# The last token tile of a Mamba block with a mixture of experts: expert picks, gate logits, ranks and GpSimd products stand elsewhere

## The reference, cut to what matters

```python
xz = einsum('bld,ed->ble', x, W_in); xs, z = split(xz)
xc = silu(causal_conv4(xs) + conv_b)
a = softplus((xc @ W_x.T)[..., :32] @ W_dt.T + b_dt)
out = (xc * a * silu(z)) @ W_out.T + x
x1 = layernorm(x + out)
scores = sigmoid(x1 @ gate_w.T); sfc = scores + gate_bias
# 4 groups of 4 experts: the 2 groups with the largest sum of their top 2 stay,
# of those the 4 best experts; their weights are scores, normalized, times 2.5
y = sum over the token's experts e of cw[e] * (silu(x1 @ Wg[e].T) * (x1 @ Wu[e].T)) @ Wd[e].T
y += (silu(x1 @ Ws_g.T) * (x1 @ Ws_u.T)) @ Ws_d.T
x2 = layernorm(x1 + x1 + y)
```

## Time and profile before

| | us |
|---|---|
| median of 3 runs | 582.47 (579.99 to 583.5) |
| the profiled execution | 584.27 |
| its span on the core | 582.5 |
| TensorE busy | 527.9 (91%) |
| VectorE busy | 434.3 (75%) |
| ScalarE busy | 373.3 (64%) |
| GpSimd busy | 332.1 (57%) |

### The profile page before, as it was taken

One profiled execution on the slowest core, in us unless ns is written; L12 is line 12 of the kernel. 1 busy time (PEld: TensorE's weight loads), 2 busy tenths in 40 slices (PEclk: granted clock), 3 DMA queues, 4 the chain that ended last, 5 costly groups with the idle time before them and its releaser, 6 DMA issues.

```text
span 582.5 us, 11734 instructions
## 1 busy us (share of the span) xinstructions
PE 527.9 (91%) x3112; PEld 442.9 (76%) x3112; DVE 434.3 (75%) x1103; ACT 373.3 (64%) x960; POOL 332.1 (57%) x368
## 2 busy tenths in 40 slices
PE   6878899899999999999859898999999998899782
PEld 5667486686867778676648798899999998889661
DVE  4886599998999999999895577434353558887666
ACT  4693858858486683855622576677777776676561
POOL 2412113277575766856576667777777766666720
PEclk9988999999999999999988999999999999999997
DMA  7992403234142422313695647977676688883986
GB/s 163 309 292 81 153 36 110 73 120 152 62 148 83 154 98 94 132 52 108 214 384 189 225 155 245 329 243 220 195 212 196 196 302 289 294 299 128 360 316 228
DMA packets 70182, 111.21 MB, mean 191 GB/s; under 512 B 12676, under 2 KB 52997, under 8 KB 69608
## 3 DMA queue, kind: packets, MB, share of 16 engines
q1 hardware_dynamic: 53624, 71.38, 38.7%
q0 software_dynamic: 13056, 35.68, 16.7%
q10 hardware_dynamic: 3440, 3.41, 1.7%
HBM read 61.77 MB, written 50.74 MB: 193 GB/s over the span
## 4 chain that ended last, share of the span: by engine, by line
PE 46%; DVE 31%; issue 10%; ACT 5%; DMA 4%; POOL 3%; POOLq 0%; SPq 0%; ACTq 0%; DVEq 0%
PE psum L928 6%; DVE xc L1366 6%; PE psum L929 5%; PE psum L930 5%; PE psum L910 5%; PE psum L731 4%; DVE sp L1388 3%; PE psum L952 3%; PE psum L954 3%; PE psum L953 3%; PE psum L938 2%; POOL x_buf L620 2%; DVE m L1392 2%; PE psum L706 2%; PE psum L670 1%
## 5 line engine op out<-in xcount | busy, mean ns | idle before, releaser
L620 POOL DMA_INDIRECT x_buf<-row,row_id x128 | 131.4, 1026 | 64.6 <-issue 36.2
L662 POOL DMA_INDIRECT y_buf<-y_out,y_ids x96 | 95.8, 998 | 47.1 <-issue 26.9
L612 POOL TENSOR_TENSOR m<-xc,zs 128x512 f32<-128x512 f32 x32 | 41.5, 1317 | 90.1 <-DVE shift L1428 44.5
L1736 DVE TENSOR_TENSOR t_lo<-psum,t_hi 128x512 fp32r<-128x512 f32 x72 | 48.8, 685 | 55.6 <-ACT t_hi L1215 55.6
L928 PE MATMUL psum<-ew_gu_hi,t_hi 128*128 x288 | 84.8, 295 | 2.6 <-issue 0.8
L929 PE MATMUL psum<-ew_gu_lo,t_hi 128*128 x288 | 81.7, 284 | 0.0
L930 PE MATMUL psum<-ew_gu_hi,t_lo 128*128 x288 | 81.4, 283 | 0.0
L1366 DVE SCALAR_TENSOR_TENSOR xc<-psum,cw_taps,xc 128x511 f32<-128x511 f32 (+2 forms) x96 | 71.5, 747 | 7.2 <-ACT halo_x L1055 4.9
L928 PEld LDWEIGHTS psum<-ew_gu_hi,t_hi 128*128 128x128 f32 x288 | 54.8, 190 | 6.8 <-issue 5.8
L731 PE MATMUL psum<-wout,m 128*128 128x256 f32 x224 | 53.2, 398 | 3.7 <-DVE m L1392 3.1
L929 PEld LDWEIGHTS psum<-ew_gu_lo,t_hi 128*128 128x128 f32 x288 | 55.0, 191 | 0.2
(11 more groups left out here) (241 smaller groups left out, 1347.6 us busy)
## 6 DMA issues: line engine op xcount, KB each, us to landing
tiles_in<-x_buf SPq DMA_DIRECT2D x144, 144.0 KB
y_in<-y_buf SPq DMA_DIRECT2D x32, 512.0 KB, 6.2
xT<-in_x_T SPq DMA_DIRECT2D x8, 512.0 KB, 3.7
xtok<-in_x_tok SPq DMA_DIRECT2D x8, 512.0 KB, 3.6
gu_hi_buf<-w_hi_now SPq DMA_DIRECT2D x8, 512.0 KB, 3.7
out_dram<-res ACTq DMA_DIRECT2D x6, 512.0 KB, 5.6
x_buf<-pad_row SPq DMA_DIRECT2D x17, 144.0 KB
raw_gu<-in_wg_T SPq DMA_DIRECT2D x16, 128.0 KB, 3.6
```

Source lines behind the costliest of these rows:

```text
L620: nc.gpsimd.indirect_dma_start(out=x_buf, out_offset=bass.IndirectOffsetOnAxis(ap=row_id[t % ROWS][:, b, k:k + 1], axis=0), in_=row[t % RO ...
L662: nc.gpsimd.indirect_dma_start(out=y_buf, out_offset=bass.IndirectOffsetOnAxis(ap=y_ids[:, q % IDS, i:i + 1], axis=0), in_=y_sent[:, i, :] ...
```

## The change

Five edits, all on the last tile:

1. GpSimd: ahead of chunks 2 and 3 of tile 7's product the wait for `y_done` is gone. The waits for `wout_mm`, `xc_done` and `z_evac` stay.
2. `gate(7)` writes its logits to PSUM bank 4, which held the turned rows of tile 7 and is free once the gate's inputs are read; `gate_out(7)` reads them there. `gate_turn` still writes to bank 3.
3. So `gate(7)` no longer waits for `routed` = 7. That wait now stands ahead of `gate_turn(7)`.
4. TensorE: `ranks(6)` stands behind `gate_up(0, 0)`, `gate(7)` and `turn_x(0, 1)`, directly ahead of `shared_up(7, 0)`.
5. VectorE: `pick(6)` stands behind the layer norm, `shared_act(6, 1)` and the low parts of the first quad; `x1T_low(7)` stands ahead of `choose(6)`.

```diff
--- before.py
+++ after.py
@@ -381,6 +381,10 @@
             if c < 2:
                 return 4 + c
             return c - 2 if t == NT - 1 else 4 + c if t == 0 else 2 + c
+
+        def gate_bank(t):
+
+            return 4 if t == NT - 1 else 3
 
         def z_bank(c):
 
@@ -632,7 +636,8 @@
 
             def tile(t, sends=True, first=False, halos=True, last=False):
                 if not first:
-                    at_least(pool, "y_done", PAIRS * t + 1)
+                    if not last:
+                        at_least(pool, "y_done", PAIRS * t + 1)
                     gate_product(t, range(2, KI))
                 if sends:
                     send(t - 2, range(0, 2))
@@ -758,9 +763,7 @@
                 at_least(pe, "x1T_h", KD * (t + 1))
                 at_least(pe, "x1T_l", KD * (t + 1))
                 at_least(pe, "z_evac", KI * min(t + 2, NT))
-                if t == NT - 1:
-                    at_least(pe, "routed", t)
-                o = psum[0:2 * E, 3, :]
+                o = psum[0:2 * E, gate_bank(t), :]
                 for k in range(KD):
                     pe.matmul(o, gw_split[:, k, :], x1T_hi[:, k, :], start=k == 0, stop=False)
                     mm = pe.matmul(o, gw_split[:, k, :], x1T_lo[:, k, :], start=False, stop=k == KD - 1)
@@ -1006,11 +1009,12 @@
             shared_up(t - 1, 1)
             transposes(t)
             shared_down(t - 1)
-            ranks(t - 1, t)
             gate_up(0, 0, tile_experts(0))
             gate(t)
             turn_x(0, 1)
+            ranks(t - 1, t)
             shared_up(t, 0)
+            at_least(pe, "routed", t)
             gate_turn(t)
             each_quad(iteration)
             down(0, NQ - 1, tile_experts(NQ - 1))
@@ -1102,7 +1106,7 @@
 
             def gate_out(t):
                 at_least(act, "logit_mm", t + 1)
-                A(logits[:, :], psum[0:2 * E, 3, :], ACT.Copy).then_inc(s["logit_out"], 1)
+                A(logits[:, :], psum[0:2 * E, gate_bank(t), :], ACT.Copy).then_inc(s["logit_out"], 1)
 
             def gate_exp(t):
                 at_least(act, "gate_sum", t + 1)
@@ -1842,15 +1846,15 @@
                 weights_low(i)
             route(t - 1)
             shared_act(t - 1, 0)
-            pick(t - 1)
             norm_in(t, range(0, 2))
             layer_norm(t)
             shared_act(t - 1, 1)
             at_least(dve, "w_stored", 16 * PIECES)
             for k in range(KD):
                 turned_low(0, 0, k)
+            pick(t - 1)
+            x1T_low(t)
             choose(t - 1)
-            x1T_low(t)
             place(t - 1)
             residual(t - 1)
             each_quad(iteration)
```

## The result

The changed kernel takes **586.84 us** (median of 5 runs, 585.65 to 586.88) against 582.47 us (5 runs, 579.99 to 583.5): a ratio of 1.0077, 95% interval 1.0053 to 1.0102. It is slower by 4.4 us, and it lies outside the range that ended at 585.4. The profiled execution took 586.84 us, its span 585.1 us against 582.5. The lines of code have moved: L1534 was L1530, L1451 was L1447, L675 was L670, L1546 was L1542.

A forecast was written before the change was run, and what follows sets the result against it. VectorE was taken to bound the stage before tile 7's transposes, TensorE what follows. 2.6 us gained ahead of the turn and 2.6 given back behind the ranks, plus 0.4 for the clock: 582.9 us, range 579.3 to 585.4.

The forecast's parts named there:

- The picks behind the norm: VectorE, tile 6's pick: 2.13 us come out from ahead of tile 7's layer norm.
- The product without its wait: GpSimd, tile 7: second m gains 1.35 us, less 0.85 from contention with VectorE, so 0.5 us.
- one whole half: Upper bound on VectorE's delay at posn: waiting for one whole half of GpSimd's product, 1.27 us.
- The clock: TensorE's idle gaps ahead of tile 7's transposes and behind the ranks: cases -2.3, 0, +2.3 us; 0.4 added.
- As today: Likeliest of three clock cases on TensorE: slow matmuls cost the same as before, 0 us.
- The ranks behind the turn: TensorE ahead of shared_up(7, 0): the round trip to the residual, covered before, becomes bare, costing 2.6 us.
- "slower" rival: The gap ahead of shared_up(7, 0) also drops TensorE's clock, 2.3 us more: 585.2 us, chance 0.2.
- The other bank, the sends, the weights: gate(7) in bank 4, GpSimd's sends, expert weight loads: each 0 us, the weights with 3 us of cover.
- L1546 stretched to about 1 us: Sign of being right: VectorE's posn step of tile 5, held by the product; 0.22 us would mean wrong.

The follow-up runs named there:

- h2: Kernel before with only tile 6's pick moved behind the layer norm (x1T_low ahead of choose): 579.78 us, ratio 0.9934.
- f2: Kernel before with only chunk 2 of tile 7's product freed of its wait, chunk 3 keeping it: ratio 1.0004 on a 673 us chip.
- e1: Kernel before with only the wait ahead of tile 7's product (chunks 2 and 3) removed: ratio 0.998 on a 673 us chip.
- f1: Kernel before with only the wait ahead of tile 7's product removed, measured again: ratio 1.0004 on a 673 us chip.
- f3: Changed kernel plus 22 calls of unread identity products on TensorE behind the ranks: ratio 1.0073 on a 673 us chip.
- g1: The changed kernel again, unaltered, against the kernel before on another chip: 587.03 us, ratio 1.0117.
- h1: Kernel before with only the wait ahead of tile 7's product removed: 585.03 us, ratio 1.0038.
- g3: Changed kernel with tile 7's product waiting for the last step of choose(5) instead of not waiting: 583.05 us, ratio 1.0027.
- g4: Kernel before with the picks moved and tile 7's product waiting for the last step of choose(5): 578.06 us, ratio 0.9947.
- g2: Changed kernel with the product's y_done wait put back: 583.15 us, ratio 1.0017.
- i2: Kernel before with only the picks moved behind the norm: ratio 1.0068 on a 673 us chip.

## Why the prediction was wrong

- **The picks behind the norm: right, but the number it was to be seen by came out by luck.** The picks alone took the idleness ahead of the transposes from 6.29 to 3.73 us. For the whole change the forecast was 3.3 us and the measurement 3.19, though the norm was not ready 2.6 us earlier: its last step started 0.57 us later than before (302.10 against 301.53). The idle stretch shrank all the same because TensorE reached it later still. Behind `gate_turn(6)` VectorE gained the picks' 2.13 us and the whole 1.35 us at the second `m`, not 0.5, since `posn` was not held; and TensorE gained 0.43 us, since the output projection ran through, where the forecast had taken 0.4 us off the idle time for its later end. So 6.29 - 2.13 - 1.35 + 0.43 = 3.24 us, near the 3.19 measured: the two errors, each of about 0.85 us, cancel.

```profile
302.10 0.16 DVE L1432 SCALAR_TENSOR_TENSOR shift<-mv,rstd 128x4 f32<-128x4 f32 x1
```

  What the picks alone give, -0.66%, is more than the 2.1 us: the slow clock behind a shorter idle stretch costs less too (6.07 us for transposes and `shared_down(6)` in h2 against 7.10).
- **The product without its wait: this step failed.** The forecast took 0.85 us of contention at `posn` (bounds 0 to 1.27) and let nothing ahead of it suffer. It was 2.95 us, at L1534, for two reasons. It looked for the victim only among the steps that start behind the product's shown start (281.4): L1530 at 280.82 [0.22 us] was through by then. In fact the step that started 0.57 us ahead of the product's shown start was held. And the bound of "one whole half" was wrong, since the halves stand back to back and the step waited for both (3.17 us, against 1.95 with one half in f2). Behind it came what the forecast never priced: the residual of tile 5, the first thing that TensorE waits for in this stretch, with TensorE already idle for 0.90 us ahead of it. So 2.95 us went straight into TensorE's time.
- **The clock: the right mechanism at one place too few.** Two places were weighed (transposes, ranks' gap), and both showed a lower clock. The third, ahead of `shared_up(6, 0)`, cost +2.42 us, because the stall made it. "As today" held roughly for the sum of the other two: -1.38 and +1.49.
- **The ranks behind the turn: gap right, weight too small.** 2.69 us against 2.6. But the forecast booked the clock there as a rival of 0.2, at 2.3 us; it cost 1.49. Alone, this move costs 0.71%, 4.1 us. Its "slower" rival (585.2 us, to which the range adds 0.2 us without a source) was the right mechanism, and came on top of the stall that the sum did not hold.
- **The other bank, the sends, the weights: right.** No wait on weights in the changed kernel, and the sends moved without being waited for. The wait for `ew_d_hi` stays at its size:

```profile
336.28 0.38 PE L955 MATMUL psum<-ew_d_hi,a_hi 128*128 x1 [1.17 <-DMA ew_d_hi<-d_hi_buf]
```

- **What should have been asked.** The forecast's own test, "L1546 stretched to about 1 us", was refuted: 0.22 us. The product's start was given as 281.4, behind a send on GpSimd, and that was right (280.12 in an execution 1.28 us ahead). The last step of `choose(5)`, L1530 with two inputs in SBUF, lies 0.58 to 0.36 us ahead of it. No row that the forecast had said that a step so far ahead can be held, so this is hindsight; but a margin of half a microsecond around a start that is itself an estimate would have put L1530 on the list of victims. The bound would then have been 2.5 + 0.6 = 3.1 us in place of the 0.85 taken, and the range would have reached 585.4 + 2.25 = 587.6 us.

The Trainium skill, "SBUF — State Buffer", "Who interferes with whom", says that a VectorE instruction with two SBUF inputs contends with a GpSimd instruction that reads SBUF, that the shared ports are an exclusive lock, and that issue order decides who is blocked. The trace agrees (3.17 us for a step of 0.22, no delay at all for the residual with one input in PSUM). In this case's traces the step stayed blocked over two GpSimd instructions back to back.

## What to carry to other kernels

A wait that looks useless can be what keeps an instruction of GpSimd off an instruction of VectorE. Before taking it away, list every VectorE step with two inputs in SBUF from ahead of the new start (here one was held that started 0.57 us ahead of it) to its end, take the whole back-to-back run of GpSimd instructions as the price, and look at who waits behind the victim. Then add, for each idle stretch of TensorE that the change makes or lengthens, what the matmuls behind it cost at the lower clock. The better version here is the smallest: the picks behind the norm alone (0.9934), and nothing else of the change; no other version measured here had a lower ratio.

## What the runs showed of the hardware

- **A GpSimd instruction held a VectorE step that started ahead of its own shown start.** L1534 was shown from 279.55, and 0.22 us later it would have been through, 0.35 us ahead of the product's 280.12; yet it waited for it. The offset between the two shown starts was 0.57 to 0.59 us in seven kernels (changed kernel, e1, f1, f2, f3, g1, h1). The step before it, shown from 279.40 (0.72 us ahead), was not held. In g3 and g4, where the product waits for the step by a semaphore, the shown starts lie as far apart (0.59 and 0.58 us) and the step took 0.21 and 0.22 us. So it is the missing wait that made the step a victim, and the shown starts alone don't tell the two cases apart. The Trainium skill, "Perfetto Trace Analysis", "Summary: the profiler window per engine type", states that VectorE's start of reading is hidden ahead of the shown window. By that the step began to read still earlier than 279.55, so this doesn't explain the offset, and no run here shows the moment of reading itself.
- **The same idle stretch does and doesn't cost the clock.** 2.69 us ahead of `shared_up(7, 0)` left `shared_up(7, 0)` slow in the changed kernel, in g1 and in g2 (4.38 to 4.54 us), and at full clock (3.00 us) in g3's profiled execution:

```profile
314.55 0.50 PE L677 MATMUL psum<-x1T_hi,wsgu_hi 128*128 128x512 f32 x1 [2.69 <-DVE res L1453]
314.89 0.39 PE L678 MATMUL psum<-x1T_lo,wsgu_hi 128*128 128x512 f32 x1
```

- **Chips differ by 15%.** The kernel before took 672.56 us, 672.95 us and 672.99 us on three occasions and 582 us on the others. The slower chips show waits that the others don't: VectorE's 1.9 to 2.0 us at about 282 us, released by something that the profile doesn't show ("remote"), and from about 290 us on idle stretches in which the engine waited for nothing that the profile shows ("issue"). TensorE of i2:

```profile
305.22 1.97 PE L751 MATMUL psum<-ident,row 128*128 128x128 f32 x8 [6.00 <-issue]
...
331.91 0.28 PE L930 MATMUL psum<-ew_gu_hi,t_lo 128*128 x1 [1.03 <-issue]
```

There even the moved picks, a gain of 0.66% elsewhere, measured 1.0044 and 1.0068. Why these chips are slower is open.
